# Attention values as 64x32 weights in eight places of TensorE's array, with the sums by ones, in a three-layer transformer step

## The reference

```python
x = x + xattn(layernorm(x), ctx, ctx, mask, ...)   # 16 heads, 1601 keys, no softmax
x = x + attn(layernorm(x), Wq, Wk, Wv, Wo)         # 16 heads of 16, causal within 64 tokens
x = x + ffn(layernorm(x), ...)                     # rotary attention, then shared and expert MLPs

# in attn and in ffn, for every batch and head (64 queries, 64 keys, 16 values wide)
a = softmax(q @ k.T / 4)
o = a @ v          # a change of how this line is computed is the subject
y = concat_heads(o) @ Wo
```

## Time and profile before

| | |
|---|---|
| median of 3 runs | 269.75 us |
| the profiled execution, its own time | 269.39 us |
| its span | 267.6 us |
| PE busy | 241.7 us (90%) |
| PEld busy | 215.6 us (81%) |
| DVE busy | 177.3 us (66%) |
| ACT busy | 118.8 us (44%) |
| POOL busy | 69.5 us (26%) |
| mean granted TensorE clock | 0.996 |

### The profile page before, as it was taken

The page is one execution under the profiler, slowest core; times in us unless marked ns, Lnnn a source line. Parts: engine busy times, 40 slices in busy tenths (PEclk is TensorE's granted clock), DMA queues, the critical chain, the costliest instruction groups (busy, mean ns, idle before and its releaser), DMA issues.

```text
span 267.6 us, 4148 instructions
## 1 busy us (share of the span) xinstructions
PE 241.7 (90%) x1562; PEld 215.6 (81%) x1562; DVE 177.3 (66%) x373; ACT 118.8 (44%) x202; POOL 69.5 (26%) x74
## 2 busy tenths in 40 slices
PE   0988998999989999988977999999889989999991
PEld 0987998998988999967966998787658968998880
DVE  1626783776975998567966686997278556348463
ACT  4423843445176282163814599761363214541000
POOL 4011112032114004111471343797400010340010
PEclk9999999999999999999999999999999999999998
DMA  7999758585616001200001002243000000000010
GB/s 251 341 398 407 227 169 297 191 299 176 170 42 205 2 9 70 81 1 0 4 15 64 2 0 78 82 139 97 0 2 0 0 0 2 0 2 0 21 39 20
DMA packets 8419, 26.11 MB, mean 98 GB/s; under 512 B 1352, under 2 KB 2640, under 8 KB 8144
## 3 DMA queue, kind: packets, MB, share of 16 engines
q1 hardware_dynamic: 8400, 25.86, 28.8%
HBM read 25.33 MB, written 0.52 MB: 97 GB/s over the span
## 4 chain that ended last, share of the span: by engine, by line
PE 76%; DVE 7%; ACT 7%; issue 5%; DMA 2%; POOL 1%; POOLq 0%; SPq 0%; DVEq 0%; ACTq 0%
PE ps L608 70%; PE ps L611 6%; DMA raw<-in_ctx 2%; DVE prob L1108 1%; POOL rstd L394 1%; DVE mx L1107 1%; DVE Z L927 1%; ACT prob L531 1%; DVE on L1120 1%; ACT raw L464 1%; ACT L592 1%; ACT kblk L523 1%; DVE kblk L1162 1%; ACT L579 0%; ACT ks L443 0%
## 5 line engine op out<-in xcount | busy, mean ns | idle before, releaser
L608 PE MATMUL ps<-ch 128*128 128x130 f32 (+1 forms) x208 | 53.4, 273 | 7.2 <-ACT ch L495 7.2
L608 PE MATMUL ps<-ch,cl 128*128 128x260 f32 (+1 forms) x208 | 53.2, 318 | 0.0
L608 PEld LDWEIGHTS ps<-ch 128*128 128x128 f32 (+1 forms) x208 | 41.4, 199 | 7.6 <-ACT ch L495 7.2
L608 PE MATMUL ps<-w,hT 128*128 128x512 f32 x192 | 47.3, 401 | 0.0
L608 PEld LDWEIGHTS ps<-w,hT 128*128 128x128 f32 x192 | 35.7, 188 | 8.9 <-issue 0.5
L608 PEld LDWEIGHTS ps<-ch,cl 128*128 128x128 f32 (+1 forms) x208 | 41.1, 197 | 0.4 <-issue 0.2
L1022 DVE TENSOR_TENSOR cl<-raw,ch 128x1024 fp32r<-128x1024 f32 (+1 forms) x32 | 31.7, 1022 | 12.8 <-ACT ch L495 12.6
L495 ACT ACTIVATE ch<-raw 128x1024 fp32r<-128x1024 f32 (+1 forms) x32 | 27.2, 892 | 15.2 <-PE ps L608 8.2
L394 POOL TENSOR_TENSOR rstd<-ve,half_exp 128x2 f32<-128x2 f32 (+1 forms) x14 | 9.5, 677 | 78.4 <-DVE ve L899 78.2
L608 PE MATMUL ps<-xHL,dense 128*128 128x256 f32 x192 | 24.3, 284 | 1.5 <-DVE xHL L1171 1.5
L608 PEld LDWEIGHTS ps<-xHL,dense 128*128 128x128 f32 x192 | 23.3, 188 | 2.0 <-DVE xHL L1171 1.8
(11 more groups left out here) (160 smaller groups left out, 420.0 us busy)
## 6 DMA issues: line engine op xcount, KB each, us to landing
raw<-in_ctx SPq DMA_DIRECT2D x24, 512.0 KB, 3.9
raw<-in_w SPq DMA_DIRECT2D x8, 512.0 KB, 3.5
w<-in_w SPq DMA_DIRECT2D x2, 1024.0 KB, 9.2
stage<-in_dense SPq DMA_DIRECT2D x4, 512.0 KB, 6.0
mask<-in_mask SPq DMA_DIRECT2D x1, 800.5 KB, 10.4
rows<-in_rows SPq DMA_DIRECT2D x1, 768.0 KB, 8.5
raw<-in_ctx SPq DMA_DIRECT2D x8, 65.0 KB
X<-in_x SPq DMA_DIRECT2D x1, 512.0 KB, 7.2
```

The lines of the kernel that those rows point to most:

```text
L608: return pe.matmul(o, l, r, start=start, stop=stop, skip_group_check=not check)
```

## The change

- `sums` and `turn_o` are gone from the list of steps, and the tiles `sm`, `rs`, `on` and `vblk` with them.
- ACT copies the values with one plain copy for each pair of tiles into `values`, keys on the partitions, with no zeros between.
- `values` on PE: for each tile 32 products. Weights are 64 keys by 32 columns (two heads of 16) of `values`, or 64x32 ones; moving are the 128 columns of `probT` of one head pair (two parities by 64 queries). The batch of the keys gives the row half of the array (partitions 0 to 63 or 64 to 127), and the head pair one of four column strips of 32: eight places. The output is already transposed. The 16 products with ones leave the row sum in every partition of the strip. Each batch has its own PSUM bank.
- DVE takes the reciprocal of all 512 sums of a partition, multiplies, and picks the parities from SBUF, as before from PSUM.

```diff
@@ -786,18 +780,16 @@
                 elif step == "values":
                     pe.wait_ge(sem("v"), 2 * (i // 4) + i // 2 % 2 + 1)
                     pe.wait_ge(sem("probT"), 2 * i + 2)
-                    for c in range(H // 2):
-                        last = mm(ps[:, tile_bank(i), c * 4 * HD:(c + 1) * 4 * HD], probT[:, i % 2, c, :],
-                                  vblk[:, i % 2, c, :, :].rearrange("p b d -> p (b d)"), True, True)
+                    spots = [(r, bb) for r in range(4) for bb in range(2)]
+                    for part in range(2):
+                        for j in range(KC):
+                            at = (part * KC + j) * P
+                            for r, bb in spots:
+                                keys = slice(bb * S, bb * S + S)
+                                weights = const("ones")[keys, :] if part else values[keys, i % 2, 4 * j + r, :]
+                                last = mm(ps[32 * r:32 * r + 32, tile_bank(i) + bb, at:at + P], weights,
+                                          probT[keys, i % 2, 4 * j + r, :], True, True)
                     last.then_inc(sem("pv"), 1)
-                elif step == "turn_o":
-                    pe.wait_ge(sem("on"), i + 1)
-                    for bb in range(2):
-                        for j in range(KC):
-                            c = 2 * j + bb
-                            last = turn(ps[:, tile_bank(i), c * P:(c + 1) * P],
-                                        on[i % 2][:, bb, j, :, :].rearrange("p i d -> p (i d)"))
-                    last.then_inc(sem("o_turned"), 1)
@@ -1107,28 +1099,18 @@
-                elif step == "sums":
-                    k = i % 2
-                    dve.wait_ge(sem("prob"), i + 1)
-                    link(dve.tensor_reduce(sm[:, k, :], prob[:, k, :, :].rearrange("p c (b k) -> p (c b) k", b=2), AX.X, ALU.add))
-                    link(dve.reciprocal(rs[:, k, :], sm[:, k, :]))
                 elif step == "values":
 
                     k = i % 2
                     dve.wait_ge(sem("pv"), i + 1)
-                    shape = [P, H // 2, 2, 2 * HD]
-                    dve.tensor_tensor(on[k][:, :, :, :, :].rearrange("p b j r d -> p (j r) b d"),
-                                      ps[:, tile_bank(k), :].rearrange("p (c b d) -> p c b d", b=2, d=2 * HD),
-                                      rs[:, k, :].rearrange("p (c b) -> p c b", b=2).unsqueeze(3).to_broadcast(shape),
-                                      ALU.mult).then_inc(sem("on"), 1)
-                elif step == "turn_o":
-
-                    k = i % 2
-                    dve.wait_ge(sem("o_turned"), i + 1)
-                    both = ps[:, tile_bank(k), :].rearrange("p (c h q) -> p c h q", h=2, q=S)
+                    got = ps[:, tile_bank(k):tile_bank(k) + 2, :].rearrange("p b (w j n) -> p b w j n", w=2, j=KC)
+                    both = over[k][:, :, :, :, :].rearrange("p j b h q -> p b j (h q)")
+                    link(dve.reciprocal(both, got[:, :, 1, :, :]))
+                    link(dve.tensor_tensor(both, got[:, :, 0, :, :], both, ALU.mult))
+                    turned = over[k][:, :, :, :, :].rearrange("p j b h q -> p (j b) h q")
                     a = aT[k][:, :, :, :].rearrange("p j b q -> p (j b) q")
-                    link(dve.tensor_scalar(a, both[:, :, 0, :], parity(0), None, ALU.mult))
-                    dve.scalar_tensor_tensor(out=a, in0=both[:, :, 1, :], scalar=parity(1), in1=a,
+                    link(dve.tensor_scalar(a, turned[:, :, 0, :], parity(0), None, ALU.mult))
+                    dve.scalar_tensor_tensor(out=a, in0=turned[:, :, 1, :], scalar=parity(1), in1=a,
                                              op0=ALU.mult, op1=ALU.add).then_inc(sem("aT"), 1)
@@ -447,13 +445,9 @@
-            def block_values(bank):
-
-                for bb in range(2):
-                    q = slice(bb * S, bb * S + S)
-                    last = act.activation(vblk[q, :, :, bb, :].rearrange("p t c d -> p (t c) d"),
-                                          ps[q, bank, :].rearrange("p (c d) -> p c d", d=2 * HD), ACT.Copy)
-                last.then_inc(sem("v"), 1)
+            def plain_values(bank):
+
+                copy(values[:, :, :, :].rearrange("p t c d -> p (t c d)"), ps[:, bank, :], "v")
...
```

More of the change, by code:

```diff
@@ L44 @@
 for _name, _width in (("ident", P), ("parity", 2), ("heads", P), ("causal", S), ("cos", S), ("sin", S),
-                      ("rot", P), ("side", P), ("tile_of", T), ("iota", E)):
+                      ("rot", P), ("ones", 2 * HD), ("side", P), ("tile_of", T), ("iota", E)):
     CONST[_name] = (_at, _at + _width)
@@ L71, in constants @@
     put("rot", rot)
+    put("ones", 1.0)
     put("side", (p[:, None] // (P // B)) % 2 == p[None, :] // S)
@@ L110, in first_half_steps @@
         ("score", 0), ("cross4", 4), ("cross1", 5), ("gram", 19), ("score_product", 1), ("gram", 20), ("turn_p", 0),
-        ("score", 1), ("cross2_product", 5), ("sums", 0), ("cross2", 5), ("split", 22), ("turn_p", 1), ("sums", 1),
-        ("evac", 6), ("values", 0), ("values", 1), ("cross3", 5), ("turn_o", 0), ("turn_o", 1), ("piece", 1),
+        ("score", 1), ("cross2_product", 5), ("cross2", 5), ("split", 22), ("turn_p", 1),
+        ("evac", 6), ("values", 0), ("values", 1), ("cross3", 5), ("piece", 1),
         ("cross4", 5), ("cross1", 6), ("project", 0), ("project", 1), ("norm2", 0), ("gram", 21), ("gram", 22),
@@ L115, in first_half_steps @@
         ("cross3", 6), ("evac", 7), ("score_product", 2), ("score", 2), ("cross4", 6), ("cross1", 7),
-        ("score_product", 3), ("turn_p", 2), ("score", 3), ("piece", 2), ("cross2_product", 7), ("sums", 2),
-        ("turn_p", 3), ("cross2", 7), ("sums", 3), ("values", 2), ("values", 3), ("turn_o", 2), ("turn_o", 3),
+        ("score_product", 3), ("turn_p", 2), ("score", 3), ("piece", 2), ("cross2_product", 7),
+        ("turn_p", 3), ("cross2", 7), ("values", 2), ("values", 3),
         ("cross3", 7), ("project", 2), ("piece", 3), ("project", 3), ("piece", 4), ("cross4", 7), ("xo_product", 1),
@@ L130, in second_half_steps @@
         ("gate_best", 0), ("hidden", 6), ("score", 4), ("hidden", 7), ("score_product", 5), ("shared_product", 0),
-        ("shared_product", 1), ("turn_p", 4), ("piece", 7), ("experts_product", (0, 0)), ("score", 5), ("sums", 4),
-        ("piece", 8), ("turn_p", 5), ("sums", 5), ("shared", 0), ("shared", 1), ("experts", (0, 0)), ("values", 4),
-        ("values", 5), ("piece", 9), ("turn_o", 4), ("turn_o", 5), ("piece", 10), ("project", 4), ("project", 5),
+        ("shared_product", 1), ("turn_p", 4), ("piece", 7), ("experts_product", (0, 0)), ("score", 5),
+        ("piece", 8), ("turn_p", 5), ("shared", 0), ("shared", 1), ("experts", (0, 0)), ("values", 4),
+        ("values", 5), ("piece", 9), ("piece", 10), ("project", 4), ("project", 5),
         ("experts_product", (0, 1)), ("experts_product", (0, 2)), ("piece", 11), ("norm2", 1), ("experts", (0, 1)),
@@ L136, in second_half_steps @@
         ("score_product", 6), ("experts", (0, 3)), ("score", 6), ("score_product", 7), ("experts_product", (1, 0)),
-        ("turn_p", 6), ("score", 7), ("experts_product", (1, 1)), ("sums", 6), ("turn_p", 7), ("sums", 7),
-        ("experts", (1, 0)), ("values", 6), ("values", 7), ("turn_o", 6), ("turn_o", 7), ("project", 6),
+        ("turn_p", 6), ("score", 7), ("experts_product", (1, 1)), ("turn_p", 7),
+        ("experts", (1, 0)), ("values", 6), ("values", 7), ("project", 6),
         ("project", 7), ("experts_product", (1, 2)), ("rms1", 1), ("experts", (1, 1)), ("experts", (1, 2)),
@@ L227, in layer @@
     kblk, _ = place("kblk", [P, KC * BH, 4, S])
-    vblk, _ = place("vblk", [P, TH, H // 2, 2, 2 * HD])
+    values, _ = place("values", [P, TH, H // 2, 2 * HD])
     prob, _ = place("prob", [P, TH, H // 2, 2 * S])
-    on = [place(f"on{k}", [P, 2, KC, 4, 2 * HD], at=where["prob"] + k * 4096)[0] for k in range(TH)]
+    over = [place(f"over{k}", [P, KC, 2, 2, S], at=where["prob"] + k * 4096)[0] for k in range(TH)]
     aT = [place(f"aT{k}", [P, KC, 2, S], at=where["prob"] + k * 4096 + 2048)[0] for k in range(TH)]
@@ L239, in layer @@
     mx, _ = place("mx", [P, TH, H])
-    sm, _ = place("sm", [P, TH, H])
-    rs, _ = place("rs", [P, TH, H])
     hT, _ = place("hT", [P, 2, 2, HID // P, TOK], F32R)
@@ L384, in _ @@
             pool.memset(kblk[:, :, :, :], 0.0).then_inc(sem("zeros"), 1)
-            pool.memset(vblk[:, :, :, :, :], 0.0).then_inc(sem("zeros"), 1)
             pool.wait_ge(sem("ones"), CH_B + 1)
@@ L519, in _ @@
                     else:
-                        act.wait_ge(sem("zeros"), 2)
+                        act.wait_ge(sem("zeros"), 1)
                     for r in range(4):
```

4 lines of the change are left out of this document (2 added, 2 removed).

## The result

The kernel after takes 304.4 us (median of 4 runs, 301.7 to 308.7) against 269.2 us before it on the same chip: 1.125 times as long, 95% interval 1.119 to 1.131. Ratios leave out runs that lie over 1.5% above the fastest of their kernel: here the one at 308.7, later two in experiment 8 and one, at 487.4, in experiment 12. The prediction was 296 us, range 286 to 309: slower, as forecast, and 8 us above the number. The profiled execution took 301.7 us (span 299.9); the one before took 269.4 (span 267.6). So 32.3 us are to be found in the traces. DVE is busy for 195.2 us, 17.9 more than before, where the prediction had 14.

A forecast was written before the change was run, and what follows sets the result against it. The prediction took PE's queue to bound the kernel, with PE waiting for DVE behind `values`: 269.4 + 20.5 direct waits + 6.0 clock - 0.5 ACT = 295.4, given as 296 us since the runs' median lies 0.4 higher; range 286 to 309.

The forecast's parts named there:

- Direct waits behind the long reciprocal: PE waiting for DVE's 4.9 us a tile, 3.33 of it reciprocal, where `values` runs: +20.5 us together.
- the term that was to decide: DVE's reciprocal of 512 sums a tile, behind the products: 3.33 us, at 6.2 ns an element.
- 0.5 for ACT: The value copy before `score_product` becomes one instruction in place of two, one of which stood in the chain: -0.5 us.
- the second place: Where `values` runs for tiles 2 and 3; the product with `mb` behind it was forecast +4.4 us late.
- the third place: Where `values` runs for tiles 4 and 5; the experts' products behind it were forecast +4.9 us late.
- the prediction's second rival: DVE's reciprocal takes eight steps an element, 4.4 us a tile: +8.6 us together, 304 us; chance 0.13.
- PE's products: The 64 small passes of `values` a tile overlap in all eight places of the array: 1.0 us a tile.
- The rivals of half and of no overlap: PE's `values`: overlap by row halves only, +9.6, 305 us, chance 0.10; no overlap, +31, 324 us, chance 0.06.
- The clock: Lower granted clock after PE's idle waits, whole cost at the first place, half at three others: +6 us, bounds 0 and 9.
- all four places: Where `values` runs, for tiles 0 and 1, 2 and 3, 4 and 5, 6 and 7: +6.3, +4.4, +4.9, +4.9 us.
- the length of a fall: Time at the lower clock after PE idles: more than 4 us, costing up to about 2.3 us of PE work.
- The parity steps: DVE's two steps a tile after the reciprocal and multiplication: 0.41 us on 256 from SBUF, and 0.48.

The follow-up runs named there:

- experiment 8: The kernel after with only the order of steps changed, so that other PE work stands between `values` and `project`: 306.2 us.
- experiment 12: experiment 11 with the split of chunk 22 moved behind the values of tile 1: 267.0 us, ratio 0.992 to the kernel before.
- experiment 7: The kernel after with unread filler products keeping PE busy and both parity steps reading unscaled products in PSUM: 291.8 us, ratio 1.086 to the kernel before.
- experiment 6: The kernel after, long reciprocal kept, with both parity steps reading unscaled products in PSUM: 298.7 us, ratio 1.110 to the kernel before.
- experiment 1: The kernel after with the 512-element reciprocal replaced by a multiplication by 1: 286.5 us, ratio 1.068 to the kernel before.
- experiment 3: The kernel after with the first parity step written as a two-input operation, both inputs in SBUF: 304.5 us, ratio 1.130 to the kernel before.
- experiment 11: Small products kept, 16-element sums and reciprocals as in the kernel before, PE spreading the reciprocals over partitions: 266.3 us, ratio 0.989 to the kernel before.

## Why the prediction was right, and what it lacked

The spans add up: after 299.9; with the parity steps in PSUM 296.3 (-3.6); with PE kept busy as well 289.1 (-7.2); before 267.6 (-21.5). Of the last step some 1.0 us is the fillers' own (experiment 7), so by this estimate it is 20.5 for the waits and 8.2 for the clock.

- **Direct waits behind the long reciprocal**, the term that was to decide: +20.5, less 0.5 for ACT. Measured 21.5, or some 20.5 without the fillers' own. By place, from the shift of the same PE instruction between before and experiment 7: +5.6, +5.4, +4.9, +5.4, against +6.3, +4.4, +4.9, +4.9; at the second place 0.7 of the difference is the fillers'. From the start of `values` to DVE's reciprocal it took 1.28 us at the third place, predicted 1.3. A reciprocal of 512 elements took 3.35 us, where 6.2 ns an element gave 3.33; the slope between rows of 2 and of 16 elements held over a factor of 32. Eight steps at one per 1.04 ns give 4.4 us, and the trace does not agree. That was the prediction's second rival; it read the repeat count of 8 that the Trainium skill (VectorE: DVE Perf Modes, section "First, the fixed hardware budget") states as eight such steps for each element.
- **PE's products**: 1.12 us a tile and 0.99 from one tile to the next, predicted 1.0. Consecutive passes started 7 ns apart (97.021, 97.027, 97.034), eight within 0.05 us, and such groups of eight followed each other every 109 ns, the first after 133, so all eight places overlap. The rivals of half and of no overlap are out.
- **The clock**: +6 predicted, bounds 0 and 9, measured 7.2, or some 8.2 if the fillers' own time is taken off. It fell at all four places. That the number fits is in part luck. The prediction took the length of a fall, over 4 us, from the start of the kernel before, where the profile gives the granted clock as 1.00 although the passes have the long step (row below); and the stretches lasted 6.8 to 17.1 us. During the four stretches PE was busy for 23.3 us, so half of that could be lost, but part of the slow passes ran while DVE was the one waited for: the first four with `wo,aT` took 2.08 us at the second place, and the second `aT` was not ready before 152.77 anyway.

```profile
8.00:12.00 4.00, 4.00 (x20) 4.00 (x20) 1.88 (x3) 2.06 (x3) 0.00 (x0) 1.00 0.99 348
```

- **The parity steps**: the sum had 0.41 and 0.48 us for them and nothing else. Measured, two of eight first steps took 2.42 and 2.11 us and cost 3.6. This is the step that failed: "a parity step on 256 from SBUF (0.41, as the normalisation of 256)". The price was taken from a row in which nothing was held (12 steps, mean 410 ns); the change moves an operand from PSUM to SBUF, which the prediction saw only as a price and not as a wait.
- The medians are farther apart than the profiles (304.4 - 269.2 = 35.2 against 32.3): the runs after lie from 301.7 to 308.7, with clock averages from 0.923 down to 0.905, the longer the run the lower, and before from 268.3 to 270.5. So in this kernel the lower clock lasted longer in some runs than in others. It need not: the four runs of experiment 6, at 0.922 and 0.923, lie within 0.9 us.

A reader could have found the missing term. The kernel before has three held operations in its own trace, each with all its tensors in SBUF. A subtraction of 1.22 us took 1.54 at 167.76, beside POOL's; an operation on two elements took 0.49 at 159.13 in place of 0.16 and ended 0.02 us after POOL's; and a one-input step took 0.80 in place of 0.17 and ended 0.03 us after POOL's (182.71 to 185.11):

```profile
184.34 0.80 DVE L899 TENSOR_SCALAR ve<-mv 128x2 f32<-128x2 f32 x1
```

The Trainium skill (SBUF — State Buffer, section "Who interferes with whom") states that a VectorE instruction with two SBUF inputs contends with a GpSimd instruction that reads SBUF, that `tensor_scalar` from SBUF to SBUF can do so too in its two-port mode, and that there the one issued first keeps the ports for its whole instruction. The traces here agree on the first two points: tensor_scalar, tensor_tensor and scalar_tensor_tensor waited when both sides lay in SBUF, and none of 48 parity steps did in the three kernels where the operand lay in PSUM, though 18 of them ran beside an operation of POOL of over 1 us. On the order they show less. A step that started 0.05 us ahead of POOL's (200.75 in the kernel after) took its 0.48 us, and POOL's took 2.64 in place of 2.35. But two that started some 0.01 us or less ahead of POOL's took 2.63 and 2.62 us (190.70 in experiment 1, 201.44 in experiment 3).

The mechanism was right and the total 8 us low: 3.6 for the holding, 2.7 in the direct waits and the clock together, and the rest is the median of scattered runs.

## What to carry to other kernels

An operation that is spread over more partitions to save a transposition is also done more often: here 512 reciprocals of 6.2 ns took the place of 16, on the engine that everything waits for, and the gain of the quick products turned into idle time. Keep the slow function on its few elements and spread its result (experiment 11). When an operand moves from PSUM to SBUF, list POOL's operations at that time, since the DVE instruction can wait for one to its end; and behind each new idle time of PE look at the granted clock before adding up the waits.

## What was not expected

- A DVE operation of 0.35 to 0.48 us with source and destination in SBUF took up to 2.0 to 2.6 us beside POOL's two-input operation of 2.35 us. Without the reciprocal the sum of such waits was 9.8 us, and 11 us came back when the operand was read from PSUM.
- The waits do not go when POOL is moved; they go to the next instruction of that kind (`ctxT`, 0.69 to 1.98 us).
- 150 products that nobody reads made the kernel 11.8 us faster; some 2 us of that are a step that was not held.
- Bursts of 256 small passes ran into gaps of 1.7 to 3.3 us in PE's issue, at all four places, and 192 passes into one of 0.88 us behind them; beside each stands a packet of the "instruction" queue. The cause is open.
